# Two maximum tiles, of two heads, read by one VectorE instruction over two neighbouring PSUM banks

## What is computed

```
qkv = einsum('oc,bcl->bol', qkv_w, group_norm(x)) + qkv_b
weight = einsum('bhct,bhcs->bhts', q * scale, k * scale)      # 1024 x 1024 for each of 16 x 8 heads
weight = softmax(weight, axis=-1)
a = einsum('bhts,bhcs->bhct', weight, v)
```

## Time and profile before

| what | value |
|---|---|
| median of 3 runs | 1671.16 us (1671.08 to 1672.15) |
| the profiled execution: its time, its span | 1672.58 us, 1670.6 us |
| busy: PE, DVE, ACT, POOL | 1606.7, 1454.5, 1341.3, 335.6 us |
| DMA | 105.91 MB, mean 63 GB/s |
| TensorE's granted clock, mean | 0.983 of full speed |

### The profile page before, as it was taken

How to read it: one execution, slowest core, us unless ns; L and a number is a source line. 1 busy time by engine, 2 the same in 40 slices (tenths; PEclk the granted TensorE clock), 3 DMA queues, 4 the chain that set the end, 5 groups by cost and what they waited for, 6 DMA issues and landing times.

```text
span 1670.6 us, 29685 instructions
## 1 busy us (share of the span) xinstructions
PE 1606.7 (96%) x10602; PEld 673.0 (40%) x10602; DVE 1454.5 (87%) x2415; ACT 1341.3 (80%) x2478; POOL 335.6 (20%) x411
## 2 busy tenths in 40 slices
PE   4999999999999999999999999999999998899999
PEld 2433333333333333333333333333333332455555
DVE  4999999999999999999999999999999994455552
ACT  2288888888888888888888888888888887666664
POOL 3101111111111111111121212121211122322220
PEclk9599999999999999999999999999999998999999
DMA  5233333333333333333333333333333320234332
GB/s 115 32 47 59 59 59 60 59 60 59 58 61 58 60 58 61 58 61 58 61 58 60 58 61 58 49 56 50 56 50 57 50 60 29 84 115 115 88 105 75
DMA packets 58610, 105.91 MB, mean 63 GB/s; under 512 B 32864, under 2 KB 33632, under 8 KB 58464
## 3 DMA queue, kind: packets, MB, share of 16 engines
q1 hardware_dynamic: 56160, 95.64, 33.8%
q10 hardware_dynamic: 2304, 8.39, 1.2%
HBM read 34.48 MB, written 9.05 MB: 26 GB/s over the span
## 4 chain that ended last, share of the span: by engine, by line
PE 89%; ACT 4%; DVE 3%; SPq 1%; issue 1%; DMA 1%; POOL 0%; DVEq 0%; ACTq 0%; POOLq 0%
PE psum L730 31%; PE psum L714 19%; PE psum L699 15%; PE psum L843 7%; PE psum L625 4%; ACT probs L985 4%; PE psum L814 2%; PE psum L816 2%; PE psum L815 2%; PE psum L617 2%; DVE maxes L1093 2%; PE psum L662 2%; PE psum L851 1%; SPq L357 1%; DMA q_stack<-rows 0%
## 5 line engine op out<-in xcount | busy, mean ns | idle before, releaser
L1093 DVE TENSOR_REDUCE maxes<-psum 128x1 f32<-128x512 f32 x2048 | 1270.7, 681 | 54.3 <-PE psum L699 45.9
L985 ACT ACTIVATE probs<-psum 128x512 f32<-128x512 f32 x2048 | 1093.2, 601 | 199.3 <-PE psum L714 180.3
L699 PE MATMUL psum<-k_stack,q_stack 62*128 62x512 f32 x2048 | 697.9, 442 | 1.7 <-DVE maxes L1093 0.9
L714 PE MATMUL psum<-q_stack,k_stack 64*128 64x512 f32 x2048 | 691.8, 439 | 5.3 <-ACT probs L985 4.2
L730 PE MATMUL psum<-probs,values 128*32 128x512 f32 (+1 forms) x5120 | 573.7, 520 | 22.0 <-ACT probs L985 22.0
L714 PEld LDWEIGHTS psum<-q_stack,k_stack 64*128 64x128 f32 x2048 | 326.8, 186 | 322.8 <-ACT probs L985 278.3
L699 PEld LDWEIGHTS psum<-k_stack,q_stack 62*128 62x128 f32 x2048 | 333.3, 188 | 250.9 <-DVE maxes L1093 188.2
L730 PEld LDWEIGHTS psum<-probs,values 128*32 128x32 f32 x5120 | 100.8, 108 | 225.1 <-issue 140.2
L479 POOL CAST parts<-neg_max 128x16 fp32r<-128x16 f32 x64 | 12.6, 197 | 554.9 <-DVE neg_max L1072 554.9
L843 PE MATMUL psum<-probs,first_weights 128*128 128x512 f32 x256 | 116.6, 598 | 0.9 <-DVE raw L1261 0.9
L995 ACT ACTIVATE probs<-psum,params_sb 128x512 f32<-128x512 f32 x128 | 82.3, 686 | 21.3 <-PE psum L816 14.9
(11 more groups left out here) (95 smaller groups left out, 931.1 us busy)
## 6 DMA issues: line engine op xcount, KB each, us to landing
q_stack<-q_high SPq DMA_DIRECT2D x128, 128.0 KB, 4.0
k_stack<-k_high SPq DMA_DIRECT2D x128, 128.0 KB, 5.2
values<-inv_rms_rows SPq DMA_DIRECT2D x32, 512.0 KB, 5.1
x_sb<-in_x SPq DMA_DIRECT2D x16, 512.0 KB, 7.6
q_stack<-q_low SPq DMA_DIRECT2D x64, 128.0 KB, 6.3
k_stack<-k_low SPq DMA_DIRECT2D x64, 128.0 KB, 7.0
q_stack<-rows SPq DMA_DIRECT2D x512, 2.0 KB
attn<-raw SPq DMA_DIRECT2D x128, 64.0 KB, 2.3
```

What stands on the lines that cost most here:

```text
L699: nc.tensor.matmul(bank_of(max_place[tile]), q_stack[used, place, p, chunk % 4, chunk // 4, :], k_stack[used, place, p, HALF * key_half:HA ...
L714: nc.tensor.matmul(psum[:, tile % BANKS, :], k_stack[used, place, p, 128 * chunk:128 * chunk + 128], q_stack[used, place, p, :, t, :], sta ...
L985: nc.scalar.activation(probs[:, tile % 8, :], psum[:, tile % BANKS, :], ACT.Exp, scale=SCALE).then_inc(probs_ready, 1)
L1093: nc.vector.tensor_reduce(maxes[:, chunk // 4, j, 4 * p + chunk % 4, key_half:key_half + 1], bank_of(max_place[max_tile(u, s, k)]), axis=A ...
```

## The change

The banks of the ring become (3, 4, 5, 6), all neighbours; `acc` moves from bank 6 to bank 7 and `misc` from 7 to 6, and the lists of banks of the prologue and of the second block follow. In steps with even s, DVE reads tiles 0 and 1 by one reduction over 128 x 2 x 512, unless tile 0 lies in the last bank of the ring (`neighbours`). It waits for tile 1, and raises `max_taken` by 2 when it is done. Tiles 2 and 3, all tiles of odd steps, and the even steps where tile 0 lies in the last bank keep one reduction each.

```diff
-FIRST_BANKS = ((0, 1, 2, 3), (0, 1, 2, 6))
+FIRST_BANKS = ((0, 1, 2, 3), (0, 1, 2, 7))
...
-        acc, misc = psum[:, 6, :], psum[:, 7, :]
+        acc, misc = psum[:, 7, :], psum[:, 6, :]
-        HIDDEN_BANKS, CONV_BANKS, SUMS_BANK, OUT_BANK = (0, 1, 2, 7), (3, 4), 5, 6
+        HIDDEN_BANKS, CONV_BANKS, SUMS_BANK, OUT_BANK = (0, 1, 2, 6), (3, 4), 5, 7
...
-        RING_BANKS = (3, 4, 5, 7)
+        RING_BANKS = (3, 4, 5, 6)
...
+        def neighbours(n):
+            return n % len(RING_BANKS) != len(RING_BANKS) - 1
+        def two_banks(n):
+            bank = RING_BANKS[n % len(RING_BANKS)]
+            return psum[:, bank:bank + 2, :]
...
-                    for k in range(4):
-                        j, key_half, p, chunk = k % 2, k // 2, step % 2, step // 2
+                    p, chunk = step % 2, step // 2
+                    place = max_place[max_tile(u, s, 0)]
+                    in_one = s % 2 == 0 and neighbours(place) and max_place[max_tile(u, s, 1)] == place + 1
+                    if in_one:
+                        dve.wait_ge(max_ready, max_tile(u, s, 1) + 1)
+                        if step % NK == 0:
+                            at_least(dve, neg_max_ready, half_unit - 1)
+                        nc.vector.tensor_reduce(maxes[:, chunk // 4, :, 4 * p + chunk % 4, 0],
+                                                two_banks(place), axis=AX.X, op=ALU.max).then_inc(max_taken, 2)
+                        if closes:
+                            close_half(half_unit - 1)
+                    for k in range(2 if in_one else 0, 4):
+                        j, key_half = k % 2, k // 2
                         dve.wait_ge(max_ready, max_tile(u, s, k) + 1)
```

## The result

The changed kernel takes 1673.47 us (median of 20 runs), the kernel before 1671.92 us in its 20. The medians differ by 1.55 us; the ratio is put at 1.0013, with a 95% interval of 1.0007 to 1.0019, which is 2.2 us (1.2 to 3.2).

What follows compares the result with a forecast made beforehand. The prediction took PE's matmuls, with some exponentials, to bound the steady part, and DVE only the lead-in. Its terms, -0.3 (lead-in) + 0.3 (rows) + 0 (banks), sum to 0: 1671.2 us, range 1668 to 1677.

Steps and rivals of the forecast that it cites:

- What bounds the kernel: Steady part: matmuls and exponentials hold the chain, the reductions 0.4%; DVE is almost full yet in time, bounding only the lead-in.
- the sum: Whole kernel: -0.3 us (lead-in) + 0.3 (maximum rows) + 0 (banks) = 0, so 1671.2 us.
- The price of a merged instruction: DVE: a merged reduction takes 1.23 us, between 1.15 and 1.36, and saves 0.05 us of the queue.
- the first rival: Steady part: banks come back too late for PE, some 8 us slower, 1679; chance 0.19.
- The start: Steady part: DVE starts a merged reduction 0.04 us after tile 1's end, leaving margins of 0.24 and 0.25 us.
- the late start: Steady part: a merged reduction starts 0.53 us behind tile 1's start, leaving margins of 0.14 and 0.15 us.
- The step that failed: Lead-in: PE is three banks ahead, so merged instructions wait for nothing; five pairs before the transpose gain 0.3 us.
- The rival of the falling clock: New stalls drop PE's clock from 2.4 to 1.2 GHz for ten us, costing 5 us: 1676; chance 0.02.
- The maximum rows: Transpose of each half unit, then DMAs to the scores: late DVE delays the rows, taken as 0.3 us.

Runs made afterwards that it cites:

- units_0_on: Changed kernel with pairs merged only from unit 0 on, the lead-in as before: 1673.66 us, kernel before 1670.55; ratio 1.0019.
- units_1_on: Changed kernel with pairs merged only from unit 1 on, 184 of the 198: 1671.80 us; ratio 1.0006 against the kernel before.

## Why the prediction was right, and where not

*What bounds the kernel.* Right. DVE has 19.6 us less to do and nothing comes back, except in the lead-in, where the sum's -0.3 measured -0.32 (five pairs) and -0.55 (all).

*The price of a merged instruction.* 1.23 us forecast, 1226 ns measured. What a pair gives back where DVE is the bound is 0.06 us (-0.32 in five pairs, -0.55 in ten), in line with the 0.05 forecast and not with 0.135. The section of the Trainium skill that the prediction holds against this (VectorE: DVE Perf Modes, "The DRAIN you can't avoid") adds that a next instruction that isn't held starts earlier; the prediction left that out, and starts 0.598 us apart don't contradict the section as a whole. Two figures of the prediction are off without harm: 10 us is 0.7% of DVE's 1454.5 us, not 0.5%, and in the first rival DVE would be 0.42 us late by the numbers given there, not 0.3.

*The start.* I took tile 1's end plus 0.04 us. Merged reductions start 0.1 to 0.15 us behind that end. In the pair at s = 10 of unit 16, DVE and PE:

```profile
769.25 1.23 DVE L1104 TENSOR_REDUCE maxes<-psum 128x2 f32<-128x1024 f32 x1 [0.71 <-PE psum L707]
```

```profile
768.72 0.62 PE L707 MATMUL psum<-k_stack,q_stack 62*128 62x512 f32 x2
...
770.29 0.74 PE L707 MATMUL psum<-k_stack,q_stack 62*128 62x512 f32 x2
```

Tile 1 starts at 768.72 (the first of that row), DVE 0.53 us behind it, which is the late start that I kept as the bound. The banks are back at 770.48, and tile 0 of s = 11, the second of the last row, starts at 770.29 + 0.74 - 0.39 = 770.64: a margin of 0.16 us, where 0.14 was forecast for the late start. PE needs 0.05. The margin holds, except at the three places above.

*The step that failed* is "PE has written three banks ahead there, so the merged instruction waits for nothing", together with margins that were all read at the full clock. It is true up to the last tile of the lead-in. It is not true right behind it, at s = 0 of unit 0, where PE has just waited for the rows, DVE is idle, and matmuls take 0.79 us instead of 0.50. I gave that place no line of its own. It costs 0.67 us there and 1.4 us more that go with a clock that rises 3 us later.

*The rival of the falling clock* had 0.02 and was put in the steady part. What happened is akin to its mechanism, in another place: not a fall, but a later rise. The steady clock stays at 1.00, as forecast.

*The maximum rows*, +0.3 us, don't show up: the weight loads of score tiles wait for them 10 times between 200 and 1400 us, as before, 4.4 us in all and not 4.3, and the stretch of units 1 to 30 loses its 0.63 us at the three places.

*The sum* was 0, and the interval of the ratio says +1.2 to +3.2 us. By stretches the trace gives -0.32 + 2.07 + 0.63 = +2.4, of which these two executions show 0.9 in the end, because what lies ahead of the first maximum tile and behind unit 31's first score tile happened to be shorter in after. The parts of unit 0 and of the three places were left out of the sum. So the forecast of no change that can be measured held for the steady part by its reasons, and as a whole because what it left out is small against 1672 us. How much of the 1.8 us of that pair reaches the median stays open: units_0_on against units_1_on says 0.13% and all but two pairs against the change itself says the same, while the three kernels with that pair alone say 0.02 to 0.06%, with intervals that reach 0.11 to 0.14%.

## What to carry to other kernels

An engine that is 97% busy in a window can be off the critical path, as DVE is here; ask the chain and the waits, and expect nothing from making it faster except where it holds the chain. Merging two reads of this ring trades 0.05 us against a bank that comes back 0.5 to 1.3 us later: list for every instruction that takes a place, side jobs included, which one it takes over and with what margin, and do it again for the start of the pipeline, where queues are empty and the clock may be low. Two variants that I expected to cost 12 us at most cost 43 and 130 us.

## What the runs showed of the hardware

One reduction over two neighbouring banks takes 1226 ns, where two of one bank take 681 ns each and start 598 ns apart: the second bank costs 545 ns, as much as the 546 ns between DVE instructions of 512 and of 1024 elements in the earlier trace rows, so that the crossing costs nothing that can be seen.

In the five traces of kernels that merge the pair at s = 0 of unit 0, PE waits 0.33 us at the lower clock, 2.6 us behind the first score tile, and the granted clock rises 7.2 to 8.2 us behind that tile. In the nine other traces there is no such wait, and it rises 3.6 to 5.0 us behind it. That the pair does it is shown; that the wait is what counts, and not another effect of the pair, is argued.

In three places read above, 0.04 to 0.06 us lie between a bank's release by DVE and the start of the matmul that waits for it, at the lower clock (73.63 to 73.67) as at the higher one (798.92 to 798.97, 953.53 to 953.59).
